# Where the cross-attention of a four-block transformer splits the soft MoE's weights: sixteen of thirty-two units moved in the schedule

## Chip, cores and metric

The kernel runs on one core of one Trainium2 chip. The metric is the device time of one execution in microseconds (us). Three runs of the kernel before gave 1866.33, 1872.18 and 1873.15 us; the median is 1872.18 us.

## What is computed

Four blocks work on x of shape 8 x 256 x 512 (2048 rows of 512), each behind a residual addition with a tanh gate: a convolution block, a routed mixture of experts, a linear cross-attention to a context of the same shape, and a soft mixture of experts with 16 experts. The change lies in the third block. Cut to what matters:

```python
q = feature(LN(x) @ Wq.T)                    # feature: x+1 above 0, exp(x) below
gate = sigmoid(LN(x) @ Wg.T + bg)
k, v = split(ctx @ Wkv.T);  k = feature(k)   # 16 heads of 32
attn = (q @ (k.T @ v)) / (q @ k.sum() + eps)
x = x + tanh(g) * ((attn * gate) @ Wo.T)
```

The fourth block multiplies by W1 (16 x 512 x 128) and W2 (16 x 128 x 512). All products are made in float16 pairs: a float32 matrix a is kept as hi = f16(a) and lo = f16(a - hi), and a product takes three matmuls. The pairs of W1 and W2 are made ahead of the fourth block, inside the third, and kept in DRAM.

## The kernel before

`xattn_phase` works through four chunks c of 512 rows (4 tiles of 128). It writes one list, `schedule` (L1302 to L1310), of steps (chunk, operation, number), and TensorE, VectorE, ScalarE and GpSimd each walk through that list in order and do their share of each step. The engines meet only by semaphores; an engine whose instruction waits holds back everything behind it in its own order. The queue of DMAs on SP has an order of its own, written out in the sync block.

The steps of the list:

- TC, TX: TensorE turns a tile of the context or of the normalised x into a PSUM bank; ScalarE makes the hi half (c_hi L1446, x_hi L1452) and VectorE the lo half (L1553).
- K, V, KF and Q, G, QF: projections. For K and Q VectorE takes the minimum with 0 (low), ScalarE its exp (L1461, L1473), VectorE the feature (L1522), ScalarE its hi half (k_hi L1470, q_hi L1486) and GpSimd its lo half (k_lo L1399, q_lo L1404). KF of chunk c also makes GpSimd issue two gathers of expert rows for chunk c+1 (L1385). V's hi half v_hi is ScalarE's (L1467), its lo half VectorE's (L1564).
- CB, NA, NB: the earlier block's expert rows are added to x, and the layer norm.
- SM, SS: the products of keys and values, and their pair.
- AT, eight in a chunk: TensorE's products with q, then VectorE's denominator, reciprocal and product a_mixed (L1594, L1597, L1602), ScalarE's a_hi (L1496) and GpSimd's a_lo (L1408).
- OUT, four in a chunk: the output projection, which VectorE adds to x (L1606, increments out_read). Outputs 0 and 1 need the first four a_lo, outputs 2 and 3 all eight.
- P, 32 units: one splits a 128 x 512 piece of W1 (units 0 to 15) or W2 (units 16 to 31). ScalarE converts it (L1436), issues the store of unit n-1 (L1428) and the load of unit n+2 (L1419 for W1, L1421 for W2). GpSimd makes the lo half (L1396). Three buffers rotate. Ahead of the conversion ScalarE waits for the unit's load and for the store of unit n-3; ahead of the store of unit n-1 it waits for both of its halves, part_hi and part_lo (L1426, L1427).

In a chunk the list runs: Q, G, QF mixed with TC and CB of the next chunk; SM, SS; K, V, KF of the next chunk mixed with this chunk's AT, which makes four turns of K, AT, V, AT, KF; then OUT of this chunk alternating with TX of the next. "The loop" or "a turn" below means one of those four turns. Before, the 32 units stand behind each QF (16) and behind each AT of odd number (16), the latter between the turn's second AT and its KF.

SP loads the context of chunk c+1 only when it has issued the x3 stores of chunk c-1 and the context of chunk c has been turned (L1354 to L1359); each x3 store waits for its out_read (L1358).

Of the kernel before, what the change touches and what calls it, by code (L numbers as in the profile page):

```python
# [17 lines left out]
P = 128  # L18
# [33 lines left out]
def mixed(a, b):  # L52

    at = [((i + 0.5) / len(a), 0, o) for i, o in enumerate(a)] + [((i + 0.5) / len(b), 1, o) for i, o in enumerate(b)]
    return [o for _, _, o in sorted(at, key=lambda v: v[:2])]
# [1169 lines left out]
def xattn_phase(nc, k, x1s, y_rows, ctx, wq_t, wg_t, bg_cols, wkv_t, wo_t, x3, w1, w1_split, w2, w2_split):  # L1225
# [3 lines left out]
    with phase(nc) as st:  # L1229
# [62 lines left out]
        def ops(c, op, count):  # L1292
            return [(c, op, n) for n in range(count)] if c < NCH else []

        def projections(c, first, second, last, count):

            return [(c, op, n) for n in range(count) for op in (first, second, last)] if c < NCH else []

        def weights(first, end):
            return [(0, "WS", n) for n in range(first, end)]  # L1300

        schedule = (ops(0, "TC", 4) + weights(0, 2) + ops(0, "CB", 4) + ops(0, "NA", 1) + ops(0, "NB", 1)  # L1302
                    + mixed(projections(0, "K", "V", "KF", 4), weights(2, 4) + ops(0, "TX", 4) + weights(4, NP)))
# [3 lines left out]
            schedule += mixed(projections(c + 1, "K", "V", "KF", 4), ops(c, "AT", 2 * KD))  # L1307
            schedule += mixed(ops(c, "OUT", 4), ops(c + 1, "TX", 4))
        parts = iter(range(PARTS))
        schedule = [o for at in schedule for o in ([at, (0, "P", next(parts))] if at[1] == "QF" or at[1] == "AT" and at[2] % 2 else [at])]  # L1310
        assert next(parts, None) is None
        w1_d = w1.rearrange("(j e) (p k) h -> j k p e h", j=NJ, k=KD)
        w1_out = w1_split.rearrange("j p (q k d) -> j k p q d", q=2, k=KD)
# [967 lines left out]
def transformer(nc, a, out):  # L2281
# [11 lines left out]
    with ExitStack() as whole:  # L2293
# [7 lines left out]
        with ExitStack() as routed:  # L2301
            sb, _, _ = opener(nc, routed)
            k.slots, k.mix = sb("slots", [P, 2, TT], I32), sb("mix", [P, 2, TT])
            with ExitStack() as st:
                sb, _, _ = opener(nc, st)
                w = OnChip()
                k.logits = sb("router_logits", [P, TT, E])
                k.tile_expert, k.slot_token = sb("tile_expert", [P, TILES], I32), sb("slot_token", [P, TILES], I32)
                w.gate_hi, w.gate_lo, w.up_hi, w.up_lo = (sb(f"w_{n}", [P, E, KD, I_MOE], F16) for n in ("gate_hi", "gate_lo", "up_hi", "up_lo"))
                shared_phase(nc, k, w, x1, xn, x1s, a["router_t"], a[F + "gate_w"], a[F + "up_w"], a[F + "s_gate_w"],  # L2310
                             a["s_gate_b_cols"], a[F + "s_up_w"], a["s_up_b_cols"], a[F + "s_down_w"], a[F + "s_down_b"])
                w.down_hi, w.down_lo = (sb(f"w_down_{q}", [P, E, MK, D], F16) for q in ("hi", "lo"))
                route_phase(nc, k, w, a[F + "down_w"])
                expert_phase(nc, k, w, xn, expert_rows, a["L1_ffn_mu"], mu_split)
            xattn_phase(nc, k, x1s, expert_rows, flat["ctx_2048"], a["wq_t"], a["wg_t"], a["bg_cols"], a["wkv_t"], a["wo_t"], x3,
                        a["L1_ffn_W1"], w1_split, a["L1_ffn_W2"], w2_split)
# [45 lines left out]
```

## Time and profile before

| | us |
|---|---|
| three runs | 1866.33, 1872.18, 1873.15 |
| the profiled execution, time | 1872.76 |
| its span | 1870.8 |
| TensorE busy in the span | 1594.3 |
| VectorE busy | 1126.3 |
| ScalarE busy | 737.3 |
| GpSimd busy | 476.7 |
| mean granted TensorE clock | 0.933 |

The profiled execution's time has 1.96 us more than its span, and lies 0.58 us above the median. The cross-attention takes about 820 to 1178 us of the span. In the profile PE is TensorE, DVE VectorE, ACT ScalarE, POOL GpSimd; ACTq and SPq are the DMA issues of those engines. A timeline row gives start, duration, the line of the kernel and the operation; in brackets stand the idle time before it and what ended it, and a releaser named there can be one of several that the instruction waited for. DMA shares are of 16 DMA engines.

### The profile page before, as it was taken

How to read it: one execution, taken by the hardware profiler on the slowest of the kernel's cores; microseconds unless marked ns; L12 is line 12 of the kernel's file. 1: busy time of each engine (PE TensorE's matmuls, PEld its weight loads, DVE VectorE, ACT ScalarE, POOL GpSimd, SP SyncE). 2: the span in 40 equal slices, each digit the busy share in tenths (PEclk: the TensorE clock that was granted, in tenths of full speed). 3: DMA queues.
4: the chain of work that ended last, by engine and by line, in shares of the span. 5: the costliest groups of instructions: out<-in, count | busy, mean ns of one | idle time of the engine just before them, and what ended most of it. 6: DMA issues, size and time to landing. Idle time of an engine off the chain costs nothing. (4 is left out here: it accounts for less than half of the span.)

```text
span 1870.8 us, 27845 instructions
## 1 busy us (share of the span) xinstructions
PE 1594.3 (85%) x9596; PEld 929.2 (50%) x9596; DVE 1126.3 (60%) x2222; ACT 737.3 (39%) x1382; POOL 476.7 (25%) x368
## 2 busy tenths in 40 slices
PE   2989965999927999957978887588999999999997
PEld 1767752444414666633534444244555555555554
DVE  4978854555372232236868677476767677676663
ACT  2321104243321233224434433175646656465562
POOL 1223310344342344333334233112010120201000
PEclk7999987999957999978999998789999999999998
DMA  8222224323346577564243422841514225051341
GB/s 185 70 65 78 89 87 148 123 85 108 104 146 165 137 173 180 136 221 139 70 145 90 135 68 74 335 117 27 119 28 96 62 62 123 12 112 39 74 77 48
DMA packets 270075, 203.65 MB, mean 109 GB/s; under 512 B 184130, under 2 KB 220994, under 8 KB 268306
## 3 DMA queue, kind: packets, MB, share of 16 engines
q1 hardware_dynamic: 243360, 165.64, 32.6%
q0 software_dynamic: 5680, 18.62, 3.5%
q10 hardware_dynamic: 20930, 18.00, 3.2%
q8 instruction: 66, 1.08, 0.2%
q14 instruction: 39, 0.32, 0.1%
HBM read 114.57 MB, written 43.86 MB: 85 GB/s over the span
## 5 line engine op out<-in xcount | busy, mean ns | idle before, releaser
L1960 POOL TENSOR_TENSOR s_h_lo<-s_h,s_h_hi 128x512 f16<-128x512 f32 x32 | 37.0, 1156 | 552.7 <-DVE s_h_hi L2171 552.7
L274 POOL TENSOR_TENSOR prod_lo<-prod,prod_hi 128x2304 f16<-128x2304 f32 x16 | 73.3, 4582 | 168.6 <-ACT prod_hi L307 158.3
L1148 DVE TENSOR_TENSOR e_h<-e_up,e_silu 128x352 f32<-128x352 f32 x39 | 20.5, 525 | 149.6 <-ACT e_silu L1107 142.3
L463 PE MATMUL ring<-prod_hi,toep 128*128 128x288 f16 x320 | 93.4, 292 | 19.7 <-DVE terms L383 10.7
L2189 PE MATMUL s_ring<-w_mu,s_xt_hi 128*128 128x512 f16 x256 | 98.5, 385 | 4.2 <-DVE s_xt_lo L2092 3.9
L2190 PE MATMUL s_ring<-w_mu,s_xt_hi 128*128 128x512 f16 x256 | 98.5, 385 | 0.0
L2191 PE MATMUL s_ring<-w_mu,s_xt_lo 128*128 128x512 f16 x256 | 98.1, 383 | 0.0
L2189 PE MATMUL s_acc<-w_w,s_g_hi 128*128 128x512 f16 x256 | 97.1, 379 | 0.2
L2189 PE MATMUL s_ring<-w_w,s_xt_hi 128*128 128x512 f16 x256 | 97.0, 379 | 0.0
L2190 PE MATMUL s_ring<-w_w,s_xt_hi 128*128 128x512 f16 x256 | 97.0, 379 | 0.0
L2191 PE MATMUL s_ring<-w_w,s_xt_lo 128*128 128x512 f16 x256 | 97.0, 379 | 0.0
L2191 PE MATMUL s_acc<-w_w,s_g_lo 128*128 128x512 f16 x256 | 97.0, 379 | 0.0
L2190 PE MATMUL s_acc<-w_w,s_g_hi 128*128 128x512 f16 x256 | 97.0, 379 | 0.0
L2097 DVE TENSOR_REDUCE s_top<-s_lg 128x1 f32<-128x512 f32 x64 | 43.9, 686 | 88.1 <-ACT s_lg L2003 87.9
L465 PE MATMUL ring<-prod_hi,toep 128*128 128x288 f16 x320 | 93.5, 292 | 0.0
L464 PE MATMUL ring<-prod_lo,toep 128*128 128x288 f16 x320 | 93.3, 292 | 0.0
L1107 ACT ACTIVATE e_silu<-e_gate 128x352 f32<-128x352 f32 x39 | 18.1, 465 | 175.2 <-PE e_up L1052 164.5
L380 DVE TENSOR_TENSOR terms<-ring,q_e 128x512 f32<-128x512 f32 x64 | 66.8, 1045 | 26.8 <-PE ring L465 24.8
L2009 ACT ACTIVATE s_dt<-s_ring,s_slot_low 128x256 f32<-128x256 f32 x128 | 59.5, 470 | 52.4 <-DVE s_dq L2119 52.1
L2174 DVE TENSOR_TENSOR s_g_lo<-s_ring,s_g_hi 128x512 f16<-128x512 f32 x64 | 43.6, 690 | 58.7 <-ACT s_g_hi L2040 58.7
L656 POOL TENSOR_TENSOR h_lo<-h,h_hi 128x512 f16<-128x512 f32 (+1 forms) x24 | 30.9, 1287 | 179.7 <-ACT h_hi L632 179.7
L307 ACT ACTIVATE prod_hi<-prod 128x2304 f16<-128x2304 f32 x16 | 34.1, 2131 | 105.5 <-DVE prod L354 105.5
(377 smaller groups left out, 4808.5 us busy)
## 6 DMA issues: line engine op xcount, KB each, us to landing
expert_rows<-e_y SPq DMA_DIRECT2D x39, 256.0 KB
a_part_in<-in_L_ffn_W ACTq DMA_DIRECT2D x32, 256.0 KB
w_split<-a_part_q ACTq DMA_DIRECT2D x32, 256.0 KB, 2.5
w_w<-w_split SPq DMA_DIRECT2D x8, 1024.0 KB, 15.5
toep<-ssm_split SPq DMA_DIRECT2D x14, 512.0 KB, 5.2
stage<-in_L_ffn_gate_w SPq DMA_DIRECT2D x8, 704.0 KB
stage<-in_L_ffn_up_w SPq DMA_DIRECT2D x8, 704.0 KB
c_rows<-in_ctx SPq DMA_DIRECT2D x8, 512.0 KB, 11.1
```

Source lines behind the costliest of these rows:

```text
L274: nc.gpsimd.tensor_tensor(prod_lo[:, u].rearrange("p k e r -> p (k e r)"), prod[:, u, :], prod_hi[:, u].rearrange("p k e r -> p (k e r)"), ...
L380: nc.vector.tensor_tensor(to(0, (9, 4), (1, 8)), values(0, (8, 4), (1, 8)), weights(0, (0, 4), (1, 8)), ALU.mult)
L463: nc.tensor.matmul(out, w_hi, hi, start=(n == 0), stop=False)
L464: nc.tensor.matmul(out, w_hi, lo, start=False, stop=False)
L465: last = nc.tensor.matmul(out, w_lo, hi, start=False, stop=(n == m))
L1960: nc.gpsimd.tensor_tensor(hp[1][:, n % 2, :], h32[:, :], hp[0][:, n % 2, :], ALU.subtract).then_inc(S["h_lo"], 1)
L2009: last_ = A(dt[:, n % 2, e, :], ring[:, bank, e * N:(e + 1) * N], ACT.Exp, bias=slot_low[:, n % 4, e:e + 1], accum_out=slot_sum[:, 2 * n + ...
L2097: V.tensor_reduce(top[:, t, j:j + 1], lg[:, t, j * D:(j + 1) * D], AX.X, ALU.max).then_inc(S["top_done"], 1)
L2174: V.tensor_tensor(g[1][:, n % G_BUFS, :], ring[:, bank, :], g[0][:, n % G_BUFS, :], ALU.subtract).then_inc(S["g_lo"], 1)
L2189: mm(out_, a[0], b_[0], start=first, stop=False)
L2190: mm(out_, a[0], b_[1], start=False, stop=False)
L2191: return mm(out_, a[1], b_[0], start=False, stop=last_)
```

## The change

Only the condition that places the units changes:

```diff
         parts = iter(range(PARTS))
-        schedule = [o for at in schedule for o in ([at, (0, "P", next(parts))] if at[1] == "QF" or at[1] == "AT" and at[2] % 2 else [at])]
+        schedule = [o for at in schedule for o in ([at, (0, "P", next(parts))] if at[1] == "QF" or at[1] == "KF" and at[0] or at[:2] == (0, "OUT") else [at])]
         assert next(parts, None) is None
```

The units behind QF stay. Of the others, twelve stand behind the KF of chunks 1 to 3 (one in each turn of the loop, now after KF instead of before it), and four behind the outputs of chunk 0. The last chunk's AT have none. The list from the loop of chunk 0 on, before and after:

```text
before  K1.0 AT0.0 V1.0 AT0.1 P4 KF1.0 ... AT0.7 P7 KF1.3 OUT0.0    TX1.0 OUT0.1    TX1.1 ... Q1.0 .. QF1.0 P8
after   K1.0 AT0.0 V1.0 AT0.1 KF1.0 P4 ... AT0.7 KF1.3 P7 OUT0.0 P8 TX1.0 OUT0.1 P9 TX1.1 ... Q1.0 .. QF1.0 P12
before  ... QF3.3 P27 SM3 SS3 AT3.0 AT3.1 P28 ... AT3.7 P31 OUT3
after   ... QF3.3 P31 SM3 SS3 AT3.0 AT3.1     ... AT3.7     OUT3
```

The units' own instructions, their buffers and their waits are the same. The order of the units among themselves is the same too.

## Rows read from the trace of the kernel before

**Rows 1.** The page's first lines: span, then busy time and instructions of TensorE

```profile
span 1870.8 us, 27845 instructions
...
PE 1594.3 (85%) x9596; PEld 929.2 (50%) x9596; DVE 1126.3 (60%) x2222; ACT 737.3 (39%) x1382; POOL 476.7 (25%) x368
```

**Rows 2.** Stretches of the cross-attention: start, end, length, then the columns named

```profile
core 0: us, PE busy (x) PEld busy (x) DVE busy (x) ACT busy (x) POOL busy (x), PEclk, DMA share, GB/s
947.00:953.60 6.60, 6.21 (x32) 3.25 (x32) 4.02 (x7) 2.44 (x5) 4.16 (x5) 1.00 0.80 246
953.60:962.00 8.40, 2.88 (x13) 1.27 (x14) 1.46 (x3) 0.98 (x2) 0.00 (x0) 1.00 0.85 296
962.00:966.00 4.00, 4.00 (x14) 1.67 (x14) 2.31 (x4) 0.60 (x1) 0.00 (x0) 0.57 0.06 24
1001.25:1025.28 24.03, 22.23 (x123) 11.75 (x121) 20.71 (x27) 8.98 (x18) 15.82 (x17) 1.00 0.39 114
```

**Rows 3.** Timeline, TensorE, 947 to 962: start, us, instruction, idle before and releaser

```profile
947.11 0.38 PE L1619 MATMUL a_ring<-wo_hi,a_a_hi 128*128 128x512 f16 x1 [2.43 <-DVE a_feat L1522]
...
954.78 0.38 PE L1619 MATMUL a_ring<-a_xt_hi,wq_hi 128*128 128x512 f16 x1 [1.46 <-issue]
...
961.87 0.63 PE L1625 MATMUL a_ring<-ident,a_ctx 128*128 128x128 f32 x4 [4.33 <-DMA a_ctx<-in_ctx]
```

**Rows 4.** Timeline, ScalarE and its DMA issues (ACTq), one turn of the loop

```profile
1003.64 0.53 ACTq L1428 DMA_DIRECT2D w_split<-a_part_q  x1
...
1004.20 0.63 ACTq L1419 DMA_DIRECT2D a_part_in<-in_L_ffn_W  x1
1004.88 0.63 ACT L1470 ACTIVATE a_k_hi<-a_feat 128x512 f16<-128x512 f32 x1 [0.44 <-issue]
...
1007.27 0.42 ACT L1496 ACTIVATE a_a_hi<-a_mixed 128x256 f16<-128x256 f32 x1 [1.24 <-DVE a_mixed L1602]
```

**Rows 5.** Timeline, VectorE, the same turn

```profile
1003.38 0.68 DVE L1522 SCALAR_TENSOR_TENSOR a_feat<-a_ring,a_low_exp 128x512 f32<-128x512 f32 x1
...
1008.20 0.69 DVE L1564 TENSOR_TENSOR a_v_lo<-a_ring,a_v_hi 128x512 f16<-128x512 f32 x1 [0.97 <-ACT a_v_hi L1467]
```

**Rows 6.** Timeline, GpSimd, the fourth turn of chunk 0 and what follows

```profile
946.33 0.67 POOL L1408 TENSOR_TENSOR a_a_lo<-a_mixed,a_a_hi 128x256 f16<-128x256 f32 x1 [2.03 <-ACT a_a_hi L1496]
946.96 1.16 POOL L1396 TENSOR_TENSOR a_part_q<-a_part_in,a_part_q 128x512 f16<-128x512 f32 x1
948.08 1.16 POOL L1399 TENSOR_TENSOR a_k_lo<-a_feat,a_k_hi 128x512 f16<-128x512 f32 x1
...
950.66 0.95 POOL L1385 DMA_INDIRECT a_y<-expert_rows,slots  x1 [0.30 <-issue]
```

**Rows 7.** Timeline, ScalarE, the first two splits of the x transposes

```profile
947.76 1.07 ACT L1452 ACTIVATE a_xt_hi<-a_ring 128x512 f16<-128x512 f32 x2
```

**Rows 8.** Timeline, VectorE, first outputs and transposes of chunk 0

```profile
945.72 0.68 DVE L1522 SCALAR_TENSOR_TENSOR a_feat<-a_ring,a_low_exp 128x512 f32<-128x512 f32 x1
...
952.92 0.75 DVE L1606 SCALAR_TENSOR_TENSOR a_x<-a_ring,tanh_gates,a_x 128x512 f32<-128x512 f32 x1 [1.27 <-PE a_ring L1621]
953.99 0.69 DVE L1553 TENSOR_TENSOR a_xt_lo<-a_ring,a_xt_hi 128x512 f16<-128x512 f32 x1 [0.32 <-ACT a_xt_hi L1452]
```

**Rows 9.** Timeline, SP, the context load issued behind chunk 0

```profile
954.07 0.47 SPq L1355 DMA_DIRECT2D a_ctx<-in_ctx  x1
```

**Rows 10.** DMA view, 930.53 to 935: busy tenths in 40 slices, and ScalarE's queue

```profile
DMA  0000018999895165469999530000000000000000
...
q10 hardware_dynamic: 800, 0.52, 37.0%
```

**Rows 11.** Timeline, ScalarE's queue, load issues at the third QF of chunks 1 and 2

```profile
981.49 1.18 ACTq L1419 DMA_DIRECT2D a_part_in<-in_L_ffn_W  x1
...
1062.88 0.63 ACTq L1421 DMA_DIRECT2D a_part_in<-in_L_ffn_W  x1
```

**Rows 12.** Timeline, ScalarE, the last chunk's attention products

```profile
1165.26 0.42 ACT L1496 ACTIVATE a_a_hi<-a_mixed 128x256 f16<-128x256 f32 x1 [1.64 <-DVE a_mixed L1602]
```

## Prediction

> **What bounds the kernel now.** I read the page first: TensorE is busy for most of the span, and no engine is full all the time [rows 1]. That average says nothing about one stage, so I went to the stage that the edit touches, from 820 to 1178 us, and asked of each part of it which engine waits and for whom. The stretches [rows 2] separate three kinds of work. In the turns where the next chunk's keys and values run beside this chunk's attention products (1001.25 to 1025.28, three turns of 8.01 us) VectorE is busy 20.71 of 24.03 us. In the first outputs with the transposes of x (947.0 to 953.6) TensorE is busy 6.21 of 6.60 us. Then comes a hole: TensorE works 2.88 of 8.40 us, while the DMA engines are at 0.85.
>
> The rows of TensorE show the edges of that hole [rows 3]. The third output starts at 947.11, the moment after a_a_lo has its eighth piece (946.33 + 0.67, [rows 6]). The first q projection starts at 954.78, when the last x transpose has been split (953.99 + 0.69, [rows 8]). The transpose of the next context chunk starts at 961.87 after 4.33 us of waiting for the context's DMA. SP issues that DMA at 954.07 [rows 9], only after it has waited for all four out_read increments (L1358) of this chunk, the last of which comes from VectorE's addition at 952.92 + 0.75 [rows 8]. So the first outputs are bound by a loop of VectorE, ScalarE, SP and DMA, and whatever delays the fourth addition delays the chunk behind it. From 961.87 on the later stages follow each other without slack that could take a delay back: TensorE is gap-free in 962 to 966 [rows 2], then VectorE holds the turns.
>
> **The change part by part.** Sixteen of 32 units P change place: 12 go from the odd AT to the KF of the same turn (chunks 0 to 2), and four leave the last chunk's AT for the four OUT of chunk 0. From P8 on every unit therefore has an earlier slot. A unit's instructions are unchanged: on ScalarE a conversion of 0.62 us, a store issue (0.53) and, up to P29, a load issue (0.63), where the issues hold the sequencer for 0.53 + 0.63 + gaps = 1.2 us [rows 4]; on GpSimd a subtraction of 1.16 us [rows 6]. The waits move with them: store_part(n-1) waits for both halves of the unit before (L1426, L1427), the conversion waits for the load issued two units earlier and the store of three units earlier.
>
> Turns of the loop, 12 times. Before, ScalarE issues the unit's DMAs at 1003.64 and 1004.20, starts k_hi at 1004.88 and then waits 1.24 us for VectorE's product before a_hi at 1007.27 [rows 4]. After, k_hi starts when VectorE's feature ends, at 1003.38 + 0.68 = 1004.06 [rows 5], 0.8 us earlier, and the unit's 1.2 us lie behind it; the sum of ScalarE's work ahead of a_hi is the same, and the 1.24 us of slack stays. VectorE's only wait in a turn is 0.97 us for v_hi [rows 5], which is ScalarE's a_hi and v_hi after VectorE's own product; no unit lies between. k_hi and k_lo come earlier, but their first reader is SM, after all four turns. Term: 0. Bounds: if the k_hi advance of about 0.8 us reached the period, -12 x 0.8 = -10; if the unit ate all its 1.2 us in spite of the slack, +14. I take 0, since both engines' rows give the reason.
>
> The last chunk's AT. ScalarE waits 1.64 us for VectorE's product right after a unit [rows 12]. GpSimd has 0.67 of a_lo and 1.16 of the unit there in the same time, so it is ahead as well. Both are covered, and taking the four units out gives nothing. Term: 0, bounds -1 to 0.
>
> The outputs of chunk 0 (OUT0, P8, TX, OUT1, P9, ...). This is where the sum lies. P7 now stands behind KF of the fourth turn, and on GpSimd KF is k_lo and then the two gathers. Before, GpSimd runs a_lo 946.33, P7 946.96, k_lo 948.08, the second gather ends at 950.66 + 0.95 = 951.61, 3.53 us after k_lo's start [rows 6]. After: k_hi can start at 945.72 + 0.68 = 946.40 [rows 8] and ends at 947.03 (0.63, [rows 4]), k_lo starts there, gathers end at 950.56, and P7's subtraction ends at 950.56 + 1.16 = 951.7. ScalarE reaches P8 long before: its conversion is dispatched near 947.75, and behind it stands store_part(7), which waits for P7's low half until 951.7. What is queued behind that wait on ScalarE is x_hi of the first TX. Before it starts at 947.76 [rows 7]. After: 951.75 + 0.53 (store 7) + 0.63 (load 10) gives 952.93, 5.2 us later.
>
> From there I follow the order. P9 follows at once: store 8 and load 11 to 954.15, second x_hi 954.2. P10's conversion needs load 10, issued at 952.28. In a loop turn the last bytes of the pair move about 2.7 us after the load's issue (the 24th of 40 slices of 0.112 us from 930.53 on is the last one busy, [rows 10]), and I allow 0.3 for the semaphore, so it starts at 955.25; store 9 and load 12 end at 956.5, third x_hi 956.5 to 957.1, x_lo to 957.75. There VectorE makes the fourth addition at 957.75, against 952.92: +4.83. P11's two issues (from 956.6) put the fourth x_hi at 957.85 and its x_lo's end at 959.1, so the q projection starts near 959.2, +4.4. The context's DMA is issued at 954.07 + 4.83 = 958.9. That path is the later one, as before, because the context lands 7.8 us after its issue [rows 3, 9]. Term: +4.8.
>
> Contention in the same place. Four pairs of a store and a load now start within 6 us. One pair moves 0.52 MB and takes 37.0% of 4.47 us = 1.65 us of all 16 DMA engines [rows 10]. Four take 6.6 us, and the last three of the four x3 stores, now bunched into 955 to 958.5, another 0.75 MB or 2.4 us. Together 9 us of DMA work fall due between 952.9 and 958.9, so some 2 to 3 us are left when the context is issued; its first bytes take some of that time anyway. I put +1.0 on the context's landing (0 to +3), and +0.4 (0 to +1.5) on issues and landings within the chain.
>
> The Trainium skill's page "DMA: Bandwidth & Descriptors" (Issuing engines are not separate DMA queues) speaks against the new place: DMAs from the scalar, sync and gpsimd engines interleave on the same 16 engines, so the parts' transfers on ScalarE's queue do not stay out of the way of SP's context load. The trace agrees as far as it goes: in the hole the context and x loads alone have the engines at 0.85 [rows 2]. By that rule the contention term is above 0, and without it the sum would be 1.4 us smaller.
>
> The third QF. Its load issue took 1.18 us in chunk 1, where it reads W1, and 0.63 in chunk 2, where it reads W2 [rows 11]. In chunk 1 that slot now holds P14, which loads part 16, the first of W2. Bounds -0.55 to 0; I take -0.2, since the rows don't tell whether the form or the moment made it long.
>
> The clock. TensorE now idles from about 953.3 to 959.2 and again after the q projection. Before, after 4.33 us of waiting, the granted clock was 0.57 in 962 to 966 [rows 2], mostly its lower level of 1.2 GHz, costing about 4.0 x 0.43 = 1.7 us. After, the q projection may run slowly too, which the context's wait covers. Cost 0, bounds -1.7 to +1.7.
>
> Sum: 4.8 + 1.0 + 0.4 - 0.2 = +6.0 us. The profiled execution took 1872.76 us with a span of 1870.8; it lies 0.6 us above the median of 1872.18. On the median the sum gives **1878.2 us**. Chunks 1 and 2 have no unit at OUT and their P19 and P27 only swap with KF: 0.
>
> **The rivals.** *No stall to speak of*: the wait for P7's low half is short or its delay is absorbed, and the kernel stays at 1872. For it: 4.33 us of TensorE's wait look like slack. Against: the context's issue hangs on the same additions [rows 8, 9], so the wait moves along. Chance 0.08. That is also the case in which the moved units change nothing. *The loop gets shorter*: if ScalarE's earlier k_hi cut the 12 turns by 0.8 us each, the sum would be -10 + 6 = -4, or 1868; to get over 0.5% faster the 0.97 us wait would have to fall in each turn (-11.6) and the outputs cost nothing. Chance 0.04. *The outputs' DMAs choke, slower than before*: ScalarE's chain runs through load 10, load 11 and eight issues. If the loads land after 5 us instead of 2.7 (+4.6 for two), the four load issues take 1.18 instead of 0.63 us as in [rows 11] (+2.2), and the context pays 3 us, the sum is 4.8 + 4.6 + 2.2 + 3.0 = +14.6, or 1887. It counts as slower from +9.4 us on, that is from 3.4 us above my terms. Chance 0.13. *My forecast*, stall plus modest contention: 0.75.
>
> **How the numbers follow.** A measurement of this kernel can tell about 0.5%, 9.4 us, from no change. The forecast and the first rival lie within it, and the bounds of the terms give +2 to +11; the runs of before spread from 1866.33 to 1873.15. Range 1872 to 1885, which reaches into the choking case and leaves out the two lowest cases and the worst of that one. Faster 0.03 (most of the loop rival), slower 0.13, within 0.84.
>
> **What would show it.** Right: GpSimd's P7 row behind two gathers, ending near 951.7; ScalarE's first x_hi of chunk 1 at about 952.9 in place of 947.76; SP's context issue at about 959; TensorE's context transpose at 967 to 969; the turn still 8.01 us; everything behind later by about 6 us. Wrong: a turn with another period, an x_hi before 949, or a loss in the q stage of chunk 1.

## Result

Over 20 executions each, the kernel before takes 1871.59 us (median, 1866.33 to 1876.22) and the changed kernel 1876.15 us (1872.28 to 1886.67). The ratio is 1.003 with a 95% interval of 1.0019 to 1.0042: 4.6 us by the medians, 3.6 to 7.9 us by the interval, and so less than 0.5%. 1878.2 us was forecast, 6.0 us above. The profiled execution took 1877.34 us.

The page of the changed kernel, the same two lines as in [rows 1]:

```profile
span 1875.3 us, 27845 instructions
...
PE 1590.1 (85%) x9596; PEld 928.4 (50%) x9596; DVE 1125.0 (60%) x2222; ACT 738.5 (39%) x1382; POOL 475.4 (25%) x368
```

The engines do the same work; only the span differs, by 4.5 us. The rows below cut the cross-attention at the same events, above all the start of the third output of a chunk on TensorE (it waits 2.4 us for its a_lo, so it is easy to find). First SP's rows of the kernel before (first context load, first load of the next phase), then of the changed kernel:

```profile
819.74 0.41 SPq L1343 DMA_DIRECT2D a_ctx<-in_ctx  x1
...
1178.48 0.37 SPq L1884 DMA_DIRECT2D s_xln<-after_xattn  x1
```

```profile
817.93 0.40 SPq L1343 DMA_DIRECT2D a_ctx<-in_ctx  x1
...
1183.65 0.37 SPq L1884 DMA_DIRECT2D s_xln<-after_xattn  x1
```

The third outputs on TensorE in all four chunks, before (the one at 947.11 stands in [rows 3]) and changed:

```profile
1028.79 0.38 PE L1619 MATMUL a_ring<-wo_hi,a_a_hi 128*128 128x512 f16 x1 [2.43 <-DVE a_feat L1522]
...
1109.64 0.59 PE L1619 MATMUL a_ring<-wo_hi,a_a_hi 128*128 128x512 f16 x1 [2.43 <-DVE a_feat L1522]
...
1169.11 0.38 PE L1619 MATMUL a_ring<-wo_hi,a_a_hi 128*128 128x512 f16 x1 [2.44 <-issue]
```

```profile
945.71 0.38 PE L1619 MATMUL a_ring<-wo_hi,a_a_hi 128*128 128x512 f16 x1 [2.42 <-DVE a_feat L1522]
...
1033.93 0.38 PE L1619 MATMUL a_ring<-wo_hi,a_a_hi 128*128 128x512 f16 x1 [2.42 <-DVE a_feat L1522]
...
1113.18 0.38 PE L1619 MATMUL a_ring<-wo_hi,a_a_hi 128*128 128x512 f16 x1 [2.43 <-DVE a_feat L1522]
...
1172.80 0.59 PE L1619 MATMUL a_ring<-wo_hi,a_a_hi 128*128 128x512 f16 x1 [3.47 <-issue]
```

| stretch, us | before | changed |
|---|---|---|
| first context load to third output of chunk 0 | 127.37 | 127.78 |
| to third output of chunk 1 | 81.68 | 88.22 |
| to third output of chunk 2 | 80.85 | 79.25 |
| to the next phase's first load | 68.84 | 70.47 |
| the cross-attention | 358.74 | 365.72 |

The loss is in one stretch, +6.5 us behind chunk 0's outputs. One stretch is shorter by 1.6 us. The last one is longer by 1.6 us; there the changed kernel's last pair of outputs starts at TensorE's lower clock (0.59 us for the matmul at 1172.80, 0.38 for that at 1169.11 before; granted clock 0.64 in 1172.7 to 1177, 1.00 in 1169 to 1173 before). The edit takes four units out of that chunk and leaves its products alone, and a second profile of the changed kernel has 67.3 us there. In the second profiles of both kernels the stretch behind chunk 0's outputs is 86.60 us against 81.91, +4.7, and the whole stage 361.2 against 358.5. So the place of the loss repeats, and its size in one execution is known to 2 us. Ahead of the stage the changed kernel's execution was 1.8 us quicker, in phases that the edit doesn't touch; single profiles differ by a few us in that way.

Where the 6.5 us arise, on GpSimd (compare [rows 6]):

```profile
944.94 0.67 POOL L1408 TENSOR_TENSOR a_a_lo<-a_mixed,a_a_hi 128x256 f16<-128x256 f32 x1 [1.87 <-ACT a_a_hi L1496]
945.75 1.16 POOL L1399 TENSOR_TENSOR a_k_lo<-a_feat,a_k_hi 128x512 f16<-128x512 f32 x1
...
948.32 0.95 POOL L1385 DMA_INDIRECT a_y<-expert_rows,slots  x1 [0.30 <-issue]
949.28 2.28 POOL L1396 TENSOR_TENSOR a_part_q<-a_part_in,a_part_q 128x512 f16<-128x512 f32 x2
```

P7's low half no longer stands between a_lo and k_lo but behind both gathers, and it starts at 949.28. The row is two units, P7 and P8, merged. ScalarE, its queue included (compare [rows 7]):

```profile
946.48 0.63 ACT L1436 ACTIVATE a_part_q<-a_part_in 128x512 f16<-128x512 f32 x1 [0.29 <-issue]
950.54 0.53 ACTq L1428 DMA_DIRECT2D w_split<-a_part_q  x1
951.10 0.63 ACTq L1419 DMA_DIRECT2D a_part_in<-in_L_ffn_W  x1
951.83 0.60 ACT L1452 ACTIVATE a_xt_hi<-a_ring 128x512 f16<-128x512 f32 x1 [4.72 <-POOL a_part_q L1396]
...
952.55 0.63 ACTq L1419 DMA_DIRECT2D a_part_in<-in_L_ffn_W  x1
...
954.59 0.63 ACT L1436 ACTIVATE a_part_q<-a_part_in 128x512 f16<-128x512 f32 x1 [0.71 <-DMA a_part_in<-in_L_ffn_W]
...
957.79 0.63 ACT L1436 ACTIVATE a_part_q<-a_part_in 128x512 f16<-128x512 f32 x1 [1.21 <-DMA a_part_in<-in_L_ffn_W]
```

P8's conversion is over at 947.1. Then nothing until store 7 at 950.54, and the first x_hi comes at 951.83 after 4.72 us of waiting "for POOL a_part_q". Two more waits follow, for loads: P10's conversion at 954.59 and P11's at 957.79. The other ends of the chain (compare [rows 3, 8, 9]), VectorE's fourth addition, SP's context load, and TensorE's third output, first q projection and context transpose:

```profile
957.22 0.74 DVE L1606 SCALAR_TENSOR_TENSOR a_x<-a_ring,tanh_gates,a_x 128x512 f32<-128x512 f32 x1
```

```profile
958.35 0.44 SPq L1355 DMA_DIRECT2D a_ctx<-in_ctx  x1
```

```profile
960.59 0.59 PE L1619 MATMUL a_ring<-a_xt_hi,wq_hi 128*128 128x512 f16 x1 [8.66 <-issue]
...
967.09 0.63 PE L1625 MATMUL a_ring<-ident,a_ctx 128*128 128x128 f32 x4 [1.99 <-DMA a_ctx<-in_ctx]
```

From the third output (945.71) it is 11.51 us to the addition (5.81 before), 12.64 to SP's issue (6.96), 14.88 to the q projection (7.67) and 21.38 to the context transpose (14.76).

### The profile page after: what moved, and what is told of

Its sections match the earlier page's. It is cut to its first block and busy times, and to the rows that moved or that the text cites. A ratio compares the mean times of both kernels' runs of the same rounds, so it can differ in the third digit from the quotient of the medians.

```text
span 1875.3 us, 27845 instructions
## 1 busy us (share of the span) xinstructions
PE 1590.1 (85%) x9596; PEld 928.4 (50%) x9596; DVE 1125.0 (60%) x2222; ACT 738.5 (39%) x1382; POOL 475.4 (25%) x368
```

## Experiments

Times are medians, ratios are to the kernel before on the same chip, with their 95% interval. Runs on different chips are compared by their ratios. "A" is the start of chunk 0's third output.

**Only the loop's part.**

```diff
-if at[1] == "QF" or at[1] == "AT" and at[2] % 2 else
+if at[1] == "QF" or at[1] == "KF" and at[0] or at[:2] == (3, "AT") and at[2] % 2 else
```

> The kernel before with only the loop's part of the change: twelve units from the odd AT to the KF of the same turn, the last four stay at the last chunk's AT, none at OUT. Theory 1 (the loss is ScalarE's stall in chunk 0's outputs): the turn stays 8.01 us, from the start of the third output of chunk 0 on TensorE to the start of VectorE's fourth addition 5.8 us as before (11.5 after the change), to the context transpose 14.8 (21.4 after), and the time is that of before within 1.5 us. Theory 2 (the swap of unit and KF in the turns costs): the time is 4.5 us above before.

1866.24 us (12 runs), ratio 0.9973 (0.9956 to 0.9991): not the time of before, but 5 us below it by the ratio. TensorE and SP:

```profile
948.65 0.38 PE L1619 MATMUL a_ring<-wo_hi,a_a_hi 128*128 128x512 f16 x1 [2.42 <-DVE a_feat L1522]
...
961.73 0.52 PE L1625 MATMUL a_ring<-ident,a_ctx 128*128 128x128 f32 x3 [2.66 <-DMA a_ctx<-in_ctx]
```

```profile
955.61 0.57 SPq L1355 DMA_DIRECT2D a_ctx<-in_ctx  x1
```

The addition is where theory 1 wants it (5.81 us after A). But the context, issued 6.96 us after A as before, is there 6.12 us later instead of 7.80, so its transpose comes 13.08 us after A and not 14.8. Theory 2 is out, and theory 1 lacks something that makes the kernel faster.

**Only the outputs' part.**

```diff
-if at[1] == "QF" or at[1] == "AT" and at[2] % 2 else
+if at[1] == "QF" or at[1] == "AT" and at[2] % 2 and at[0] < 3 or at[:2] == (0, "OUT") else
```

> The kernel before with only the other part: the units of chunks 0 to 2 stay at the odd AT, the last four move to chunk 0's outputs. P7 then precedes the gathers on GpSimd, but P8's low half stands behind them (951.6 + 1.2 in the times of before) and store 8 waits for it. Theory 1: the stall moves from the first x_hi to the second, the fourth addition starts 9.4 us after the third output (5.8 before, 11.5 after the change), and the time is 3.5 to 5 us above before. Theory 2: 0, as before. Theory 3 (the loss is the order of P7 and the gathers alone): 5.8 and 0.

1872.86 us (12 runs), ratio 1.0012 (0.9994 to 1.003): 2.2 us above before by the ratio, 0.6 by the medians, where 3.5 to 5 were expected. The interval reaches no change. GpSimd, ScalarE, TensorE:

```profile
946.76 2.27 POOL L1396 TENSOR_TENSOR a_part_q<-a_part_in,a_part_q 128x512 f16<-128x512 f32 x2
```

```profile
945.93 0.63 ACT L1436 ACTIVATE a_part_q<-a_part_in 128x512 f16<-128x512 f32 x1 [0.69 <-DMA a_part_in<-in_L_ffn_W]
948.01 0.53 ACTq L1428 DMA_DIRECT2D w_split<-a_part_q  x1
...
949.34 0.60 ACT L1452 ACTIVATE a_xt_hi<-a_ring 128x512 f16<-128x512 f32 x1 [2.78 <-POOL a_part_q L1396]
```

```profile
942.25 0.38 PE L1619 MATMUL a_ring<-wo_hi,a_a_hi 128*128 128x512 f16 x1 [2.42 <-DVE a_feat L1522]
...
955.85 0.58 PE L1619 MATMUL a_ring<-a_xt_hi,wq_hi 128*128 128x512 f16 x1 [5.71 <-issue]
```

P7 is done ahead of the gathers, and so the first x_hi waits for no unit. P8's low half is behind them, and the second x_hi stands 2.78 us "for POOL a_part_q". The fourth addition comes 9.78 us after A (9.4 expected), the context transpose 18.49 us after it (14.76 before). TensorE doesn't wait for the context there: the q projection runs at the lower clock (0.58 us for its first matmul) until the transpose at 960.74. So the stall goes with whichever unit's low half follows the gathers; theory 3 is out. The trace has +3.7 us at the context transpose; the time only says that the loss isn't more than 5.6, and doesn't confirm one.

**The gathers moved away.** GpSimd issues chunk 2's fourth pair of gathers in the step of the last x transpose.

```diff
-                    if c < NCH - 1:
+                    if c < NCH - 1 and (c, n) != (1, 3):
                         gather(c + 1, n)
+                if op == "TX" and (c, n) == (1, 3):
+                    gather(2, 3)
```

> The changed kernel with one pair of gathers (tile 3 of chunk 2) issued by GpSimd behind the last x transpose instead of behind k_lo. Theory 1: P7's low half ends near 948.0 instead of 950.4 in the changed kernel's times, the first x_hi starts at 949.4 instead of 951.83, and what is left comes from loads 10 and 11 and from the issues: the fourth addition starts 9.1 us after the third output, against 11.5; the time is 1.5 to 2.5 us below the changed kernel. Theory 4 (the loss is the DMA traffic on the context's load): no difference to the changed kernel.

1874.68 us (12 runs), ratio 1.0011 (0.9995 to 1.0028). That is 1.5 us below the changed kernel's median of 1876.15, and 3.6 us below it by the ratios (1.003); the two intervals overlap, so the time doesn't show a gain. ScalarE, and TensorE's third output:

```profile
952.30 0.60 ACT L1454 ACTIVATE a_xt_hi<-a_ring 128x512 f16<-128x512 f32 x1 [2.28 <-POOL a_part_q L1396]
...
955.78 0.63 ACT L1438 ACTIVATE a_part_q<-a_part_in 128x512 f16<-128x512 f32 x1 [0.41 <-DMA a_part_in<-in_L_ffn_W]
```

```profile
948.61 0.38 PE L1621 MATMUL a_ring<-wo_hi,a_a_hi 128*128 128x512 f16 x1 [2.42 <-DVE a_feat L1524]
```

The first x_hi waits 2.28 us for GpSimd instead of 4.72; the fourth addition comes 9.76 us after A (9.1 expected). Without the gathers the addition is 1.75 us earlier, of the 5.7 that the change had added; the rest is the units' own chain. The first x_hi gains more, 2.43 us (3.69 us after A against 6.12), but load 10 takes 4.22 us here and 3.49 in the changed kernel, and the third x_hi stands behind its conversion at 955.78.

**The same without four loads.**

```diff
+            LEFT = (10, 11, 12, 13)
-                    if n >= 1 and n + 2 < PARTS:
+                    if n >= 1 and n + 2 < PARTS and n + 2 not in LEFT:
```

(The waits count the loads that are issued.)

> As the run before, and the loads of units 10 to 13 are left out (these four units split stale data, so a quarter of W1's pairs is not the real one). Theory 1: with no load to wait for and no load issues, ScalarE's chain is GpSimd's low halves and the store issues: the fourth addition starts 7.3 us after the third output (5.8 before), and the time is 3 to 4 us below the changed kernel, 1 to 1.5 above before. Theory 4: the traffic of four loads is gone as well, so the context lands 1 us sooner after its issue.

1871.59 us (12 runs), ratio 0.9998 (0.9978 to 1.0017). Expected were 3 to 4 us below the changed kernel and 1 to 1.5 above before; the medians have 4.6 below and 0.7 below, and the interval reaches from 4.1 below before to 3.2 above, so the time decides nothing. The trace is off too. The fourth addition comes 9.11 us after A, not 7.3. ScalarE:

```profile
945.96 0.63 ACTq L1423 DMA_DIRECT2D a_part_in<-in_L_ffn_W  x1
...
948.95 0.60 ACT L1456 ACTIVATE a_xt_hi<-a_ring 128x512 f16<-128x512 f32 x1 [1.62 <-POOL a_part_q L1396]
951.22 0.63 ACT L1440 ACTIVATE a_part_q<-a_part_in 128x512 f16<-128x512 f32 x1 [1.68 <-DMA a_part_in<-in_L_ffn_W]
```

P9 waits at 951.22 for load 9, which was issued at 945.96 ahead of the outputs: 5.26 us from issue to use. I had counted 3.0. In the changed kernel P9 reaches its load 6.6 us after the issue, so a landing as late would not be seen there. The context lands 6.24 us after its issue, against 8.92 in the run before it, whose code differs by the four loads alone: with them it lands 2.7 us later, more than the 1 us that theory 4 expected. In the DMA view of these two waits the units' queue moved 0.09 MB and 0.59 MB; the late gathers moved 0.25 and 0.52 MB, so not all of the 2.7 us need be the loads' own bytes. So the units' DMAs do have a share in the loss, besides ScalarE's stall.

**The context's load ahead of the stores.** SP loads context and x of chunk c+2 before it waits for the additions of chunk c.

```diff
-                if c < NCH - 1:
-                    sp.wait_ge(c_turned, 4 * c + 4)
-                    sp.dma_start(ctx_in[:, :, :], ctx_d[:, c * 4 + 4:c * 4 + 8, :]).then_inc(ctx_loaded, 16)
-                    load_rows(c + 1)
+                if c + 2 < NCH:
+                    load_chunk(c + 2)
```

(load_chunk(c) waits for c_turned, loads context and x of chunk c; load_chunk(1) stands ahead of the loop.)

> The kernel before with SP's order changed: the loads of context and x for chunk c+2 are issued before the x3 stores of chunk c, so they no longer wait for out_read. Theory 1 (the holes of 4.33 and 4.05 us in chunks 1 and 2 are the context's load behind the additions): both holes go, with them most of the slow-clock time behind them (1.7 us each): 8 to 12 us below before, near 1861.

1859.49 us (6 runs), ratio 0.9934 (0.9909 to 0.996): 12 us below before, the upper end of what was expected. No row of TensorE in chunks 1 and 2 waits for the context any more; A to chunk 1's third output is 75.39 us, 6.3 less than before. That settles what bound the stretch: the context's load, queued behind the additions.

> The changed kernel with the same SP order. Theory 1: the stall on ScalarE still delays the four x_hi and so the first q projection of chunk 1 (14.9 us after the third output against 7.7), and nothing hides it now: 7 to 9 us above the run before it. Theory 4 (the loss is the parts' traffic that delays the context): within 1 us of the run before it.

The units' full move on top: 1867.6 us (12 runs), ratio 0.9978 (0.9963 to 0.9993), 8.1 us above the run before. TensorE, third output and first q projection of the two:

```profile
945.53 0.38 PE L1622 MATMUL a_ring<-wo_hi,a_a_hi 128*128 128x512 f16 x1 [2.43 <-DVE a_feat L1525]
...
953.20 0.38 PE L1622 MATMUL a_ring<-a_xt_hi,wq_hi 128*128 128x512 f16 x1 [1.46 <-issue]
```

```profile
946.98 0.38 PE L1622 MATMUL a_ring<-wo_hi,a_a_hi 128*128 128x512 f16 x1 [2.43 <-DVE a_feat L1525]
...
961.81 0.59 PE L1622 MATMUL a_ring<-a_xt_hi,wq_hi 128*128 128x512 f16 x1 [8.61 <-issue]
```

7.67 us against 14.83, and A to chunk 1's third output is 84.78 against 75.39. The two intervals don't overlap. With the context out of the way the stall shows undiluted, in the trace and in the time. Theory 4 as the only cause is out.

For the third variant SP no longer issues load_chunk(1) ahead of the loop:

```diff
                 if n == 1:
                     load_rows(0)
+                if n == 3:
+                    load_chunk(1)
```

> The kernel of e5_ctx_first with the load of chunk 1's context and x issued behind the fourth weight piece instead of behind the eighth. Theory 1: the hole of 7.7 us ahead of 879.66 goes as well, at least in part, since the weight pieces behind it then land later: 4 to 9 us below e5_ctx_first, near 1854.

1856.38 us (7 runs), ratio 0.9941 (0.9914 to 0.9967). The hole ahead of chunk 1's first transpose is gone, but behind it TensorE now waits for a_kv_lo longer than the 2.40 us of the kernel before:

```profile
901.46 0.37 PE L1623 MATMUL a_ring<-a_q_hi,a_kv_hi 128*128 128x256 f16 x1 [6.56 <-DVE a_kv_lo L1590]
```

The median is 3.1 us below e5_ctx_first, less than the 4 expected, and the ratios (0.9941 and 0.9934, same chip) stand the other way round. A gain over e5_ctx_first isn't shown.

**Why is the loop's part faster?** Two theories, four more runs with fresh profiles, and one that combines. The first:

```diff
-                    if c < NCH - 1:
+                    if c < NCH - 1 and n < 3:
                         gather(c + 1, n)
+                        if n == 2:
+                            gather(c + 1, 3)
```

> The kernel before, all units in their old places, but GpSimd issues the fourth turn's pair of gathers already behind the third turn's pair, 8 us earlier. In the run of e1_loop_only the context landed 6.12 and 6.69 us after its issue in chunks 1 and 2, against 7.80 and 7.51 in the kernel before, and the time was 6 us lower. Theory G (gathered rows in flight ahead of the context's load delay it, and the unit behind KF lets the gathers go out 1.1 us earlier): the context lands 6.0 to 6.7 us after its issue here too, and the time is 3 to 6 us below before. Theory U (the units' own transfers or chance made the difference): landing 7.5 to 7.8 us, the time of before.

SP's context load and TensorE's transpose of it, in the run with all units in their old places and only the fourth pair of gathers earlier:

```profile
954.10 0.43 SPq L1355 DMA_DIRECT2D a_ctx<-in_ctx  x1
```

```profile
960.01 0.63 PE L1627 MATMUL a_ring<-ident,a_ctx 128*128 128x128 f32 x4 [2.45 <-DMA a_ctx<-in_ctx]
```

5.91 us, and 5.64 in the next chunk. On the landing theory G is right: with every unit in its old place, earlier gathers alone bring the context sooner. (The fourth pair is issued 5.9 us earlier, its first gather 3.61 us ahead of A instead of 2.28 behind it, and not 8.) On the time it isn't borne out: 1870.6 us (12 runs), ratio 0.9993 (0.9977 to 1.0008), where 3 to 6 us less were expected. GpSimd pays there: a_lo of the fourth turn stands behind four gathers and comes 0.4 us late in chunks 0 and 1. That explains 1 us at most. The profile alone would mislead here. It shows 78.45 and 77.75 us for the stretches of chunks 1 and 2 (81.68 and 80.85 before), but its execution was the fastest of the twelve (1866.34).

> The kernel of e1_loop_only once more, to see whether its time below before and its landing times repeat. Theory G: landing 6.0 to 6.8 us in both chunks, 1868 or less with before at 1871.5. Theory of chance: landing up to 7.8 us, the time of before.

1868.02 us (13 runs), ratio 0.9981 (0.9967 to 0.9996). The gain repeats, smaller than the first time: 3.5 us by the ratio, 2.8 by the medians (before has 1870.81 here). The forecast of the time holds to 0.02 us, that of the landing doesn't: 7.09 us behind chunk 0, above the 6.8 expected. The profiled execution was the slowest of the thirteen (1876.21).

> The kernel before, a second profile: how much do the stretches vary from one execution to the next? Theory G: the context lands 7.2 to 8.0 us after its issue in both chunks; theory of chance: anywhere from 6 to 8.

> The changed kernel, a second profile. From the third output of chunk 0 to the fourth addition 11.0 to 11.6 us, to the first q projection 14.4 to 15.0, to the context transpose 20.5 to 21.5; in chunk 2 the context lands 6.7 to 7.0 us after its issue (7.5 in before) by theory G.

The second profiles (1870.52 and 1876.72 us in one execution each) repeat the first ones closely. From A to the addition, the q projection and the context transpose: 5.81, 7.67, 14.94 us in the kernel before, 11.54, 14.96, 21.32 in the changed one. From SP's issue of the context to TensorE's transpose, in all profiles where SP's order is the old one:

| kernel | loaded behind chunk 0 | behind chunk 1 |
|---|---|---|
| before, two profiles | 7.80, 7.98 | 7.51, 7.28 |
| outputs' part only | 7.58 (TensorE busy until then) | 7.22 |
| loop's part only, two profiles | 6.12, 7.09 | 6.69, 6.37 |
| changed, two profiles | 8.74, 8.64 | 6.91, 5.72 |
| changed, late gathers | 8.92 | 5.84 |
| the same without four loads | 6.24 | 5.95 |
| early gathers | 5.91 | 5.64 |

With the unit ahead of KF it is 7.2 to 8.0; with the unit behind KF, the gathers in their usual place and no units at the outputs 5.7 to 7.1. For the changed kernel behind chunk 1, 6.7 to 7.0 was expected of the second profile, and 5.72 is outside; the 7.2 to 8.0 expected of the second profile of before were met. In the profile with 5.72 the outputs of chunk 1 ran slowly and SP's issue came 1.7 us later, so the gathers had still more time. That isn't all of it: in the profile with 7.09 the outputs ran slowly too and the issue came equally late. What makes the landing late isn't shown either. In the 9 us behind the context's issue at chunk 0 the gathered rows were 0.07 and 0.18 MB in the two profiles of before, 2.0% and 4.9% of the DMA engines' time (0.2 and 0.4 us); they were 0.05 MB and nothing with the loop's part only, and nothing with early gathers. Those rows' own time is less than the 1 to 2 us at stake.

**Both together.** The kernel of e7_ctx_first_both with the loop's units behind KF.

> The kernel of e7_ctx_first_both with the units of the loop behind KF as in e1_loop_only. Alone that move gave 0.27% and 0.19% in its two measurements. Theory G (its gain is the earlier landing of the contexts of chunks 2 and 3, which no one waits for here any more): within 2 us of e7_ctx_first_both, near 1857, and no wait of TensorE for the context behind the first one. Theory U (the gain is in the turns or on ScalarE): 3 to 5 us below e7_ctx_first_both.

1856.02 us (6 runs), ratio 0.9918 (0.9892 to 0.9943), and no wait of TensorE for the context behind the first one. The medians have 0.4 us between this and e7_ctx_first_both (1856.38), which is what theory G expects. The two ran on different chips, and by the ratios (0.9918 and 0.9941) this one is 4.3 us lower, which is what theory U expects; the intervals overlap. So the run doesn't decide between them. With f1_early_gather: that the gathers' moment moves the landing is shown; that the gain in time comes from there is not. It has the lowest median here, 15 us below before.

## Why the prediction was right, and where not

**The turn, 0: right.** The same reciprocal of VectorE in two turns running, 8.01 us apart, and ScalarE's slack, in the changed kernel (compare [rows 4]):

```profile
1010.16 1.75 DVE L1597 RECIPROCAL a_denom<-a_denom 128x256 f32<-128x256 f32 x1
...
1018.17 1.75 DVE L1597 RECIPROCAL a_denom<-a_denom 128x256 f32<-128x256 f32 x1
```

```profile
1009.23 0.63 ACT L1470 ACTIVATE a_k_hi<-a_feat 128x512 f16<-128x512 f32 x1 [0.18 <-DVE a_feat L1522]
...
1012.41 0.42 ACT L1496 ACTIVATE a_a_hi<-a_mixed 128x256 f16<-128x256 f32 x1 [0.82 <-issue]
```

k_hi follows VectorE's feature at once, and ScalarE still stands idle for 0.82 us ahead of a_hi. The row names "issue", but VectorE's product ends at 1012.37 and a_hi starts at 1012.41, so it is that product that it waits for. The prediction had the slack of 1.24 us unchanged; it shrank to 0.82 and was enough.

**What the turn's swap does elsewhere: missed.** The prediction wrote of k_hi and k_lo that "their first reader is SM". It followed GpSimd's arithmetic and not what GpSimd issues next in the same step: the gathers go out earlier as well. By the rows it is 0.94 us: the second gather stands 2.61 us behind the third output, at 948.32, and stood 3.55 behind it before, at 950.66 [rows 3, 6] (the expectations say 1.1 us). The runs put the whole swap at 3.5 to 5 us less (0.9973 and 0.9981). The earlier landing accounts for some 1 us in each of two chunks. The rest isn't shown; the stretches at the lower clock behind the context's wait differ by 1.7 us between profiles of one kernel, and may hold it.

**The stall, +4.83 at the addition and +0.4 for issues and landings: right in kind, +5.70 in size.** P7's low half was to end 5.4 us after a_lo's start (946.33 to 951.7 in the times of before); it ended 5.5 us after (944.94 to 949.28 + 2.28 / 2 = 950.42). The first x_hi was forecast 5.8 us after the third output and came after 6.12. What is mis-sized is the load: 3.0 us from issue to conversion, where load 10 took 3.49 (951.10 to 954.59), load 11 5.24 (952.55 to 957.79) and, in the run without loads, load 9 5.26. The rows of DMA activity that gave 2.7 us show when bytes move in a turn of the loop, not when the waiting engine goes on beside four such pairs and the x3 stores. The 0.3 us allowed for the semaphore has no row of its own; it is inside these 3.5 to 5.3 us.

**Contention on the context, +1.0: right as a number, by two effects that the prediction didn't part.** 8.74 us from issue to use against 7.80, +0.94. The context is issued later in the changed kernel and the gathers earlier, so the first of the fourth pair lies 11.3 us ahead of the context's issue, and lay 4.7 ahead before. With early gathers alone, 10.6 us ahead, the landing was 5.91. Read so, from single profiles, the units' transfers cost the context 2.8 us and the gathers' distance gave 1.9 back. In the DMA view of the changed kernel from 958.35 to 967.09 the units' queue takes 30.3% of the DMA engines' time, 2.6 of 8.74 us. The Trainium skill's page "DMA: Bandwidth & Descriptors" (Issuing engines are not separate DMA queues) says that the transfers of all issuing engines share the DMA engines; the trace agrees, with 8.92 us for the context beside the four loads and 6.24 without them (both with late gathers). The prediction's reading that context and x loads "alone" have the engines at 0.85 in the hole was not exact: the DMA view of 953.6 to 962 gives SP's queue 77.3%, with the last x3 store in it, and the gathered rows 7.4%. Summed over the place the terms were 6.2 us, the trace has 6.62 (6.38 in the second profiles).

**The third QF, -0.2: not there.** The load of W2 in that slot takes as long as W1's did:

```profile
986.70 1.11 ACTq L1421 DMA_DIRECT2D a_part_in<-in_L_ffn_W  x1
```

1.11 us against 1.18, so the form of the load isn't what made it long.

**The clock, 0: right.** The q and the g projection of chunk 1 in the changed kernel, stretches as in [rows 2]:

```profile
core 0: us, PE busy (x) PEld busy (x) DVE busy (x) ACT busy (x) POOL busy (x), PEclk, DMA share, GB/s
960.60:965.10 4.50, 4.50 (x12) 1.47 (x12) 0.00 (x0) 0.00 (x0) 0.00 (x0) 0.60 0.93 308
967.00:971.00 4.00, 3.92 (x13) 1.70 (x14) 1.84 (x3) 0.60 (x1) 0.00 (x0) 0.57 0.21 79
```

The granted clock is 0.60 and 0.57. The q projection is slow now, and the context's wait covers it (1.99 us are left of it); the g projection is as slow as before (0.57). From the context transpose to chunk 1's third output it is 66.84 us against 66.92; in the second profiles 65.28 against 66.97, so the clock can give back 1.7 us in one execution, the bound that the prediction had set.

**The last chunk, 0: right.** The changed kernel's last stretch, third output of chunk 2 to the next phase, is 67.3 us in its second profile and 70.5 in its first; in all the other profiles it is 67.3 to 68.9, whether there are units in it or not.

In sum +6.2 at the outputs was close. The net of 4.6 us (5.6 by the ratio) is smaller, and the gain of the other twelve units has the sign to make up the difference. Its size, 3.5 to 5 us measured alone, is too large for that: 6.6 less the gain would be 1.6 to 3.1 us, and the interval starts at 3.6. In the changed kernel the context behind chunk 0 lands no earlier than before (8.74 us), only that behind chunk 1 does, so part of the gain can't show; whether that closes the sum no run tells. That the forecast of the total came so close is in part luck, since a gain of several us was left out of it. Of the rivals, the one without a stall fell with the trace, the choking one with the interval, which ends 7.9 us above before (9.4 were its threshold), although a load did take over 5 us as it said (5.24), and the shorter loop was right that the swap gains, by a way that it did not name.

## What to carry to other kernels

When a unit of background work moves past a step, list everything that the step issues on every queue, not only what it computes: here the same gathers made the move cost more at one place (a low half stuck behind them) and less at another (issued sooner, they let the next large load land sooner). A wait that is harmless at a distance of a whole turn, the store of unit n-1 for its low half, becomes a chain when units stand a few us apart. And where a load hangs behind stores in one queue, look at the order of that queue first: it was worth 11 to 15 us here, and the places tried for the small work about 5.

## What the hardware showed beyond that

A load of 256 KB took from 3.5 to 5.3 us between issue and first use, though in a turn of the loop its bytes moved within 2.7 us. And the load of 1 MB of context behind the outputs took 5.6 to 8.9 us from issue to use: 5.6 to 5.9 with the gathers 5.9 us earlier, 8.6 to 8.9 behind chunk 0 in the changed kernel and with late gathers. That spread of 3.3 us is over half of the change that was measured.
